# Cross attention in a three-stage decoder: side work in small pieces inside the sampling slots, and positions and row norms on GpSimd

## The reference

```
K, V = context @ Wk.T + bk, context @ Wv.T + bv         # 16 heads of 16 features
Qp   = x @ Wq.T + bq
off  = Qp @ Woff.T + boff                               # 5 offsets for each token and head
loc  = mod(ref + off + token, length - 1)
ix   = ((loc / 76 * 2) * 77 - 1) / 2;  x0 = floor(ix);  dx = ix - x0
sk, sv = 0.5 * ((1 - dx) * K[x0] + dx * K[x0 + 1]), the same of V
ctx  = softmax_5(Qp . sk / 4) . sv
x    = norm(x + ctx @ Wo.T + bo)
```

## Time and profile before

| | us |
|---|---|
| median of 3 runs | 2189.01 (2186.74 to 2196.78) |
| the profiled execution | 2185.08 |
| its span, first to last instruction | 2183.2 |

### The profile page before, as it was taken

How to read it: one execution, slowest core, us unless ns; L and a number is a source line. 1 busy time by engine, 2 the same in 40 slices (tenths; PEclk the granted TensorE clock), 3 DMA queues, 4 the chain that set the end, 5 groups by cost and what they waited for, 6 DMA issues and landing times. The chain is left out here.

```text
span 2183.2 us, 42277 instructions
## 1 busy us (share of the span) xinstructions
PE 1855.1 (85%) x16907; PEld 1112.6 (51%) x16907; DVE 1614.8 (74%) x2224; ACT 1310.0 (60%) x1718; POOL 1405.9 (64%) x1059
## 2 busy tenths in 40 slices
PE   6889999999999999999999996587887788873675
PEld 3445545555555545555554544365665666652332
DVE  6776786787787786796787742679778778689676
ACT  3555666665665665666666651476856756783466
POOL 0766876977887887787787771355555455535346
PEclk8999999999999999999999997799988998996786
DMA  7013213203312212311320212000000000100002
GB/s 239 20 35 79 65 34 78 64 16 78 74 33 71 64 42 53 86 48 43 76 61 22 64 26 60 7 8 2 3 7 2 2 2 2 44 2 1 2 1 77
DMA packets 57507, 92.32 MB, mean 42 GB/s; under 512 B 25313, under 2 KB 35553, under 8 KB 53345
## 3 DMA queue, kind: packets, MB, share of 16 engines
q1 hardware_dynamic: 48096, 89.36, 15.9%
q10 hardware_dynamic: 9216, 0.27, 0.2%
HBM read 51.33 MB, written 4.46 MB: 26 GB/s over the span
## 5 line engine op out<-in xcount | busy, mean ns | idle before, releaser
L947 POOL TENSOR_TENSOR acc<-acc,probs 128x1024 f32<-128x1024 f32 (+3 forms) x320 | 585.0, 1828 | 103.5 <-ACT probs L650 72.9
L650 ACT ACTIVATE probs<-psum 128x1024 f32<-128x1024 f32 (+3 forms) x384 | 290.6, 812 | 162.2 <-PE psum L501 160.0
L594 ACT ACTIVATE chunks<-psum 128x1024 bf16<-128x1024 f32 x288 | 282.0, 1026 | 123.5 <-PE psum L460 77.9
L1505 ACT ACTIVATE onehot<-psum 128x1024 bf16<-128x1024 f32 x320 | 323.1, 1038 | 1.3 <-PE psum L1315 1.3
L493 PE MATMUL psum<-operands 64*128 64x512 f32 (+3 forms) x1536 | 306.7, 511 | 17.4 <-ACT chunks L594 16.9
L801 DVE TENSOR_REDUCE lows<-chunks 128x2 f32<-128x1024 bf16 (+1 forms) x224 | 266.8, 1217 | 73.3 <-ACT chunks L594 63.4
L1912 POOL TENSOR_TENSOR vs<-vs,wgt 128x1280 f32<-128x1280 f32 x64 | 156.4, 2444 | 248.2 <-DVE wgt L1756 248.1
L517 PE MATMUL psum<-probs,vals 128*64 128x512 f32 (+3 forms) x1536 | 295.7, 502 | 22.6 <-POOL probs L926 12.0
L1333 PE MATMUL psum<-pieces,onehot 128*128 128x64 bf16 x7680 | 287.8, 198 | 25.4 <-ACT vs L1512 18.0
L1333 PEld LDWEIGHTS psum<-pieces,onehot 128*128 128x128 bf16 x7680 | 259.5, 101 | 87.1 <-issue 44.5
L926 POOL TENSOR_SCALAR_AFFINE_SELECT probs<-probs 128x256 f32<-128x256 f32 x256 | 149.4, 601 | 125.2 <-ACT probs L650 125.1
(11 more groups left out here) (230 smaller groups left out, 3348.3 us busy)
## 6 DMA issues: line engine op xcount, KB each, us to landing
operands<-turned SPq DMA_DIRECT2D x124, 256.0 KB, 5.1
rden<-inverse_rows SPq DMA_DIRECT2D x64, 256.0 KB, 4.0
raw<-in_wqk SPq DMA_DIRECT2D x30, 256.0 KB, 4.3
y<-in_x SPq DMA_DIRECT2D x1, 4096.0 KB, 17.8
wo<-in_wo SPq DMA_DIRECT2D x16, 256.0 KB, 2.6
out<-res SPq DMA_DIRECT2D x16, 256.0 KB, 2.1
raw<-in_wv SPq DMA_DIRECT2D x15, 256.0 KB, 4.4
raw<-in_xT SPq DMA_DIRECT2D x12, 256.0 KB, 4.1
```

Of the source, the lines that this page charges most:

```text
L594: nc.scalar.activation(chunks[k % MBUF][:, :, :], slot("max", n, c)[:, :, :], ACT.Copy, scale=-1.0)\
L650: nc.scalar.activation(probs[u % PBUF][:, :, 0:width], slot("s", n, u)[:, :, 0:width], ACT.Exp, scale=1.0 / D ** 0.5).then_inc(s_exp, 1)
L947: G.tensor_tensor(dst, dst, src, ALU.add).then_inc(s_acc, 1)
L1505: A.activation(onehot[:, n % 2, k, :], bc[m % 2], ACT.Relu).then_inc(s_oh, 1)
```

## The change

**Pieces.** Each kind of side work is cut into pieces of at most 256 columns (`RIDERS`: 8 for x1T, cT, q and out, 4 for off, kv and i0), and each piece has a place (`RIDERS_AT`) with a sample. It doesn't take a slot of its own: it is written into 128 columns of each bank behind the 320 that the sample has (`seat`), by PE just before the sample. PE waits for the slot once, ahead of the piece. DVE reads a piece after waiting for the sample in the same slot (the read and the sample would touch the same bank), and before the products; ACT copies a piece after the values. Queries, keys, values and the output projection are now in products of 128 columns, instead of 256 or 512. `tT` becomes two tensors, x1T and outT.

**Positions.** `locate` has 12 steps; the two sums of reference point and token are one table made once, added where the offsets are read. For batches 1 to 3 it runs on POOL, in 13 instructions: steps 0 to 5 ahead of the batch's first whole round of `weigh_values`, steps 6 and 7 ahead of the second, 8 to 11 ahead of the third. For batch 0 it stays on DVE.

**Norms.** The normalising of rows (8 instructions of 256 columns for each batch) moves from DVE to POOL for all batches but the last one's second norm. The first norm of batch 3 moves from batch 2's sampling to batch 0's.

**Biases.** The two biases that POOL adds come in 4 instructions of 512 columns each.

**Keys.** Bias and scale are one DVE operation from PSUM per piece, with the scaled bias made once, instead of a sum and two scalings.

The core of the diff; `count` is the number of pieces of a kind done by then, and `seat` is the slot's columns 320 to 447. The functions that are not shown (transposes, copies, the residual) change in the same way as `project_kv` and `project_q`:

```diff
-FIRST_UNITS = [("x1T", 0), ("x1T", 1), ("fold", 0), ("off", 0), ("kv", 0), ("q", 0), ("q", 1), ("i0", 0)]
-EARLIER_AT = {(4, 0): ("cT", 0), (4, 2): ("cT", 1), (5, 0): ("out", 0), (5, 2): ("out", 1)}
-LATER_AT = {(6, 0): ("x1T", 0), (6, 2): ("x1T", 1), (7, 1): ("kv", 0), (8, 1): ("off", 0),
-            (10, 0): ("q", 0), (10, 2): ("q", 1), (14, 3): ("i0", 0)}
-LOCATE_AT = [(9, 2), (9, 3), (10, 1), (10, 3), (11, 1), (11, 3), (12, 1), (12, 3), (13, 1), (13, 3)]
+RIDERS = {"x1T": KT * TILE_PAIRS, "fold": 1, "off": TILE_PAIRS, "kv": 4, "q": TT, "i0": NHP // 2, "cT": KT * TILE_PAIRS,
+          "out": TT}
+FIRST_RIDERS = ["x1T", "fold", "off", "kv", "q", "i0"]
+RIDERS_AT = {"x1T": [(0, 0), (0, 1), (0, 2), (0, 3), (1, 0), (1, 1), (1, 2), (1, 3)],
+             "off": [(2, 0), (2, 2), (3, 0), (3, 2)],
+             "kv": [(5, 0), (5, 2), (6, 0), (6, 2)],
+             "q": [(9, 0), (9, 2), (10, 0), (10, 1), (10, 2), (11, 0), (11, 1), (11, 2)],
+             "i0": [(14, 0), (14, 1), (14, 2), (15, 0)],
+             "cT": [(2, 1), (2, 3), (3, 1), (3, 3), (4, 0), (4, 1), (4, 2), (4, 3)],
+             "out": [(5, 1), (5, 3), (6, 1), (6, 3), (7, 0), (7, 2), (8, 0), (8, 2)]}
+LENGTHS_AT = (3, 1)
+LOCATE_PARTS = 12
+LOCATE_BY_POOL = [range(0, 6), range(6, 8), range(8, LOCATE_PARTS)]
+BIAS_PARTS = 4
+X1_STATISTICS_AT = [(0, 1), (0, 2)]
+X1_AGGREGATE_AT = (0, 3)
+X2_STATISTICS_AT = [(7, 1), (9, 2)]
+X2_AGGREGATE_AT = (9, 3)
             for u in range(UNITS):
-                use = unit_at(b, h, u)
-                if use:
-                    order.append(use)
-                order.append(("s", H * b + h, u))
-    return order + [(kind, XB - 1, i) for kind, i in LAST_UNITS]
+                rider = rider_at(b, h, u)
+                order.append(([rider] if rider else []) + [("s", H * b + h, u)])
...
-                wait_slot("s", n, u)
+                if not rider_at(b, h, u):
+                    wait_slot("s", n, u)
...
-            def project_kv(b):
+            def project_kv(b, i):
+                v, s = divmod(i, 2)
                 pe.wait_ge(s_in, 32 * (b + 1))
-                wait_slot("kv", b, 0)
-                dst = slot("kv", b, 0)
-                for v in range(2):
+                wait_slot("kv", b, i)
+                dst = seat("kv", b, i)
+                for half in range(2):
+                    c = s * E + half * P
                     for kt in range(KT):
-                        last = nc.tensor.matmul(dst[:, v, :], ctxT[:, v, kt, :], wkv[:, kt, :],
+                        last = nc.tensor.matmul(dst[:, half, :], ctxT[:, v, kt, :], wkv[:, kt, c:c + P],
                                                 start=kt == 0, stop=kt == KT - 1)
                 last.then_inc(s_kv, 1)
...
+            def project_q(b, t):
+                pe.wait_ge(s_x1Tc, count("x1T", b, KT * (t // 2) + KT - 1))
+                wait_slot("q", b, t)
+                dst = seat("q", b, t)
+                for half in range(2):
                     for kt in range(KT):
-                        last = nc.tensor.matmul(dst[:, t // 2, t % 2 * E:(t % 2 + 1) * E], tT[:, kt, tok:tok + P],
-                                                wq[:, kt, :], start=kt == 0, stop=kt == KT - 1)
+                        last = nc.tensor.matmul(dst[:, half, :], x1T[:, kt, t * P:(t + 1) * P],
+                                                wq[:, kt, half * P:(half + 1) * P], start=kt == 0, stop=kt == KT - 1)
                 last.then_inc(s_qd, 1)
...
                 for u in range(UNITS):
-                    use = unit_at(b, h, u)
-                    if use and use[0] == "i0" and n + 1 < HEADS_ALL:
+                    if n + 1 < HEADS_ALL:
                         for k in AHEAD[u]:
                             make_onehot(n + 1, k)
-                        copy_unit(*use)
-                    else:
-                        if use:
-                            copy_unit(*use)
-                        if n + 1 < HEADS_ALL:
-                            for k in AHEAD[u]:
-                                make_onehot(n + 1, k)
                     copy_values(n, u)
+                    rider = rider_at(b, h, u)
+                    if rider:
+                        copy_unit(*rider)
                 if j == SOFT_AT and r:
                     exps(r - 1)
...
-            def scale_kv(b):
...
+            def set_kv_scales():
                 for v in range(2):
                     for s in range(2):
-                        ins = V.tensor_scalar(kvd[:, :, 2 * s + v, :], kvt[:, s, :].rearrange("p (h d) -> p h d", d=HD),
-                                              valid[:, v:v + 1], 0.5 if s else 0.5 * HD ** -0.5, ALU.mult, ALU.mult)
+                        st.then(V.tensor_scalar(kv_scale[:, v, s:s + 1], valid[:, v:v + 1], 0.5 if s else 0.5 * HD ** -0.5,
+                                                None, ALU.mult))
+                        st.done(V.tensor_scalar(kv_bias[:, v, s, :], bkv[:, s * E:(s + 1) * E], kv_scale[:, v, s:s + 1],
+                                                None, ALU.mult))
+                st.settle()
+            def scale_kv(b, i):
+                v, s = divmod(i, 2)
+                dve.wait_ge(s_kv, count("kv", b, i))
+                if i == 0:
+                    dve.wait_ge(s_pieces, b)
+                V.scalar_tensor_tensor(out=kvd[:, :, 2 * s + v, :].rearrange("p (a h) d -> p a h d", a=2),
+                                       in0=seat("kv", b, i).rearrange("p a (h d) -> p a h d", d=HD),
+                                       scalar=kv_scale[:, v, s:s + 1],
+                                       in1=kv_bias[:, v, s, :].rearrange("p (a h d) -> p a h d", a=2, d=HD),
+                                       op0=ALU.mult, op1=ALU.add).then_inc(s_kvr, 1)
...
+            def read_off(b, tp):
+                dve.wait_ge(s_off, count("off", b, tp))
+                tiles = slice(2 * tp, 2 * tp + 2)
+                V.tensor_tensor(dx[b % 2][:, tiles, :], seat("off", b, tp)[:, :, 0:HK], table[:, tiles, :], ALU.add)\
+                 .then_inc(s_offr, 1)
...
                 if part == 0:
-                    dve.wait_ge(s_offr, b + 1)
+                    dve.wait_ge(s_offr, RIDERS["off"] * (b + 1))
                     dve.wait_ge(s_len, b + 1)
-                    st.then(V.tensor_tensor(c, a, over(ref.unsqueeze(1), [P, TT, HK]), ALU.add))
-                    st.done(V.tensor_tensor(a, c, over(loc.unsqueeze(2), [P, TT, HK]), ALU.add))
+                    st.done(V.tensor_scalar(c, a, inv, MAGIC, ALU.mult, ALU.add))
                 elif part == 1:
-                    st.then(V.tensor_scalar(c, a, inv, MAGIC, ALU.mult, ALU.add))
                     st.done(V.tensor_scalar(d, c, MAGIC, size, ALU.subtract, ALU.mult))
                 elif part == 2:
-                    st.then(V.tensor_tensor(c, a, d, ALU.subtract))
-                    st.done(V.tensor_scalar(d, c, inv, 0.0, ALU.mult, ALU.is_lt))
+                    st.done(V.tensor_tensor(c, a, d, ALU.subtract))
                 elif part == 3:
-                    st.then(V.tensor_scalar(e, d, size, None, ALU.mult))
-                    st.done(V.tensor_tensor(a, e, c, ALU.add))
+                    st.done(V.tensor_scalar(d, c, 0.0, size, ALU.is_lt, ALU.mult))
                 elif part == 4:
-                    st.then(V.tensor_scalar(c, a, 1.0 / (M - 1), float(M), ALU.mult, ALU.mult))
-                    st.done(V.tensor_scalar(a, c, 0.5, None, ALU.subtract))
+                    st.done(V.tensor_tensor(a, c, d, ALU.add))
                 elif part == 5:
-                    st.then(V.tensor_scalar(c, a, MAGIC, MAGIC, ALU.add, ALU.subtract))
-                    st.done(V.tensor_tensor(d, c, a, ALU.is_gt))
+                    st.done(V.tensor_scalar(c, a, 1.0 / (M - 1), float(M), ALU.mult, ALU.mult))
                 elif part == 6:
-                    st.then(V.tensor_tensor(e, c, d, ALU.subtract))
-                    st.done(V.tensor_tensor(a, a, e, ALU.subtract))
+                    st.done(V.tensor_scalar(d, c, 1.0, MAGIC, ALU.subtract, ALU.add))
                 elif part == 7:
-                    st.then(V.tensor_tensor(c, e, e, ALU.mult))
-                    st.done(V.tensor_scalar(d, c, SQUARE_STEP, SQUARE_STEP, ALU.add, ALU.subtract))
+                    dve.wait_ge(s_i0t, RIDERS["i0"] * b)
+                    st.done(V.tensor_scalar(row, in_pairs(d), MAGIC, None, ALU.subtract))
                 elif part == 8:
-                    dve.wait_ge(s_i0t, b)
-                    for n, src in enumerate((e, d)):
-                        st.done(V.tensor_copy(i0b[:, :, :, HP * NK * n:HP * NK * (n + 1)],
-                                              src.rearrange("p t (g n) -> p t g n", g=NHP)))
+                    st.done(V.scalar_tensor_tensor(out=in_pairs(a), in0=in_pairs(c), scalar=-0.5, in1=row,
+                                                   op0=ALU.add, op1=ALU.subtract))
+                elif part == 9:
```

(46 more changed lines are left out.)

415 lines of the change are left out of this document (222 added, 193 removed).

## The result

The changed kernel takes 2131.8 us (median of four runs, 2131.5 to 2136.2), the kernel before 2187.9 beside it: a ratio of 0.9746, 95% interval 0.9728 to 0.9764, or 56 us faster. The forecast was 2100 with 2085 to 2120 as its own range and 2065 to 2142 over the cases. The result lies in the wide range, outside the likeliest case's own, nearest to rival B (2137). The profiled execution of after took 2131.5 us (span 2129.6), so the two traces differ by 53.6 us of span, and these are what the following adds up.

A forecast was written before the change was run, and what follows sets the result against it. It took a ring without slack as the bound, ACT full and PE close behind; sampling -74.4, preparation -15 and tail +2 gave -87.4, 2101.6 on the median's scale, forecast 2100 us; range 2085 to 2120, over the cases 2065 to 2142.

The forecast's parts named there:

- the likeliest case: Whole kernel: the forecast itself, 2100 us with 2085 to 2120 as its range; chance 0.55.
- rival B: Sampling: pieces help nothing, each rider adds its full time (+25), port and tail cost more; about 2137 us; chance 0.20.
- The bound: Sampling: a ring without slack rather than one busy engine; an undisturbed batch 107.4 us, riders some 50 and 54 more.
- The pieces' fraction: Full batches: 0.7 of the riders' 28.1 us is added, 19.7 us; bounds 0.38 and 1.0.
- Preparation: Ahead of the sampling: a shorter chain of DVE operations, -15 us, bounds -8 and -18.
- GpSimd's prices: POOL in a batch: positions 14.5 us, row norms 3.6, about 20 us more with waits, lying beside other work.
- Rival C: Sampling: GpSimd ends last and delays the gathers; at 5 us an instruction the kernel takes about 2260 us; chance 0.06.
- Port and DVE's reads: Full batches: softmax waiting beside POOL adds 3 us a batch, DVE's new PSUM reads add 3 us.
- Batch 0: First batch's sampling: no out parts, no softmax in its first round; 122.4 us, -16.0.
- The tail: After the sampling: transposed and projected pieces go one behind the other over two slots; +2 us, bounds -1 and +6.
- ACT's wait for products: Sampling, a sign of being right: ACT's wait for DVE's products, 143.4 us before, down by half.
- Heads 5, 6, 10 and 11: Sampling, a sign of being wrong: these heads above 10 us would show that pieces help nothing.

The follow-up runs named there:

- e6: The changed kernel with the matmuls of each query piece of batches 1 to 3 issued twice: 2152.0 us.
- e7: The changed kernel with only the first of two accumulating steps of each query piece in batches 1 to 3, so half their matmuls left out: 2128.5 us.
- e12: The changed kernel with a sampling slot's readers swapped: ScalarE copies as soon as the sample is there, VectorE multiplies behind it: 2115.3 us.
- e1: The changed kernel with GpSimd's one-input position instructions and row norms written without subtract, the one comparison kept: 2131.9 us.
- e4: The changed kernel without GpSimd's positions of batches 1 to 3 (only the last instruction stays), which sample at batch 0's positions: 2126.1 us.
- e10: The changed kernel with offset, outT and query pieces and lengths placed earlier, one-input position steps begun with a multiplication by one, norms as multiply-add: 2138.3 us.

## Why the prediction was right and wrong, step by step

**The bound: right.** The prediction called the kernel a ring without slack, in which riders cost their time, and so it is.

**The pieces' fraction: the step that failed most.** "I take 0.7" should have been 1.0, the upper bound. PE's price was right: batch 1 has 121.1 us of PE busy, 31 above four undisturbed rounds' 90.1, of which some 2 are head 12 at the lower clock; 28.1 was forecast. But the 17.4 us of PE's idle time in a batch are no room: of them 16.7 were left in batch 1 (137.83 less 121.10), where the prediction had 8.4 of them used. Some 7.4 stand in the four heads ahead of which a softmax is made; in the heads with query pieces they are the wait for a one-hot that ACT makes after it waited for the product, and a piece moves both. e6 shows it piece by piece, e7 in head 9 but not in the whole, e12 shows what the constant is. Only heads 5 and 6, with a piece in every unit, used the wait up. On 84.4 us of riders the 0.3 are 25.3 us. Rival B named this mechanism at this price; it was wrong in adding the port and the tail, and whether its headline holds, that pieces help nothing against whole units, no run tests.

**Preparation: -8.0 instead of -15**, the lower bound. The sum of DVE's operations was right, two waits weren't. Three offset pieces came 1.7 us apart, because PE's granted clock was 0.50 there, and DVE waited 0.94 + 1.38 + 1.38. And the last six steps stood beside POOL's split: from 1375.39 to 1386.24, 10.9 us for operations that sum to 4.1 at 0.55 (one input) and 0.82 (two); the first of them, the third and the fifth:

```profile
1375.39 1.45 DVE L1713 TENSOR_SCALAR off<-off 128x640 f32<-128x640 f32 x1
...
1378.12 2.64 DVE L1718 SCALAR_TENSOR_TENSOR dx<-off,i0b 128x640 f32<-128x640 f32 x1
...
1382.37 2.29 DVE L1723 TENSOR_SCALAR i0b<-off 128x640 bf16<-128x640 f32 x1
```

**GpSimd's prices: wrong, and it didn't matter.** 21.9 + 9.8 us a batch instead of 14.5 + 3.6, but the cover held: POOL still waited 105 us for weights, inside the forecast's 100 to 150, and e1 and e4 put what it cost at 0 and at 1 to 2.5 us a batch. Two-input instructions of the positions took 1.25 to 1.54, a little under the 1.62 counted. The one-input price came from DVE's and one of the feed forward, without a look at which operation it was. The Trainium skill ("GPSIMD Engine Reference", Engine selection) puts a one-input operation near line rate; the 0.73 to 0.80 us of those that begin with a multiplication, against DVE's 0.55, is not far from it, the 1.8 to 2.4 of the others is, and the measurement decides. Rival C was far off: it needed 3.9 us for each instruction, and they average 1.5 (31.7 us for 21).

**Port and DVE's reads: +6 a batch was too much.** 107.4 + 28.1 = 135.5, and batch 1 took 137.8, so both together with the clock's fall in head 12 are 2.3.

**Batch 0: 136.2 instead of 122.4**, half of the miss in the batches. The fraction explains 5.5 of it. The rest is mostly the granted clock, 0.77, 0.69 and 0.66 in heads 0, 1 and 8: PE was busy for 119.9 us where four undisturbed rounds and the riders are 108.6; and with the same work in heads 0 and 1, e4's took 9.22 and 8.50 us at 0.83 and 1.00, after's 9.80 and 10.89. What makes it fall in one kernel and not in another there wasn't settled; batches 0 of 131.3 (e10), 131.9 (e4) and 124.7 us (e12) have fewer such stretches.

**The tail: 0 instead of +2**, within its bounds (and a part that differs by up to 7 us between traces).

Together: -87.4, plus 25.3 for the fraction, 7 for the preparation, about 8 for batch 0's clock, 1.4 for the later start of the cross attention, less 7 for port and reads in batches 1 and 2 and less 2 for the tail, is about -55; the traces differ by 53.6.

Of the signs named beforehand: the full batches took 137.8 and 138.3, just over 130 to 137; POOL's wait of 105 us and its 21.9 us of positions were within theirs (right); heads with two query pieces 8.2 (near 8: right); DVE at most 6.3 busy in heads 9 and 10 (right); ACT's wait for products fell by a fifth, not by half (wrong, and the sign of the ring that e12 opened); the first sample at 1395 instead of 1387. The clock in heads 7 and 8 of batch 1 is 1.00 (0.76 over that stretch in the earlier trace rows), and over batches 1 and 2 it rose from 0.90 and 0.89 to 0.98 and 0.96: in batch 1 it falls in heads 12 and 13, in batch 2 in heads 4, 8 and 12. In batch 0 it went the other way, from 0.95 to 0.90, and head 8 there had 0.66, the sign of being wrong that the prediction named. Heads 5, 6, 10 and 11 stayed under 10 us, although B's mechanism held: that test was set too coarse, since full price is 9.35 us for head 5.

## What to carry to other kernels

Idle time of an engine in a ring is room for more work only if the wait in it doesn't move along with the work: look who ends the wait, and test with the piece issued twice before counting a fraction. Where two engines read the same buffer in turn, try letting the one go first whose next work others wait for; here it was worth more than any shift of the pieces. Compare the stretch that was changed as well as the whole time: in e7 and e10 the rest of the kernel differed by 5 and 7 us by itself. What a placement wins in one head can be lost in another where TensorE's clock is lower, so it is judged by whole batches, not by its best heads.

## What the runs showed of the hardware

GpSimd's price of a one-input instruction with two scalars depends on the operations. In after and e1, for 128 x 640 float32: multiply-add 0.80, multiply-multiply 0.75 and add-multiply 0.80 us, but subtract-multiply 2.43, less-than-multiply 2.43, add-add 2.37, a single addition 1.83 and a single subtraction 1.86; a row norm of 256 columns 1.22 as subtract-multiply and 0.58 as multiply-add. A multiplication by one ahead of the single addition brings it to 0.73 (e10).

TensorE's granted clock fell to 0.50 behind heads in which it had waited (2.67 busy of 4.49 us ahead of the fall in head 12), and the stretch that pays is a busy one: PE was busy for 6.14 of the next 6.80 us, with 30 matmuls at 1.78 us instead of 1.05, and in e10 a whole head of 14.62 us ran at 0.53, busy throughout, behind a wait of 1.36.
